# The variance of a channel norm on 64 columns instead of 128, and what spreads it back

## The chip, the core and the metric

The kernel runs on one core of a Trainium2 chip. The core has a TensorE (PE, 128x128 array, with its weight loads shown apart as PEld), a VectorE (DVE), a ScalarE (ACT), a GpSimd (POOL) and a SyncE (SP) that issues transfers. The metric is the time of one execution on the device in microseconds; less is better.

## The reference, cut to what matters

The input x is (4, 64, 32, 32): four images, 64 channels, 1024 positions each. It goes through a convolutional local attention (7x7 windows) on a channel norm of x, is added to x, and the sum goes through a sequence of attention and feed-forward steps on a channel norm of that, and is added again:

```python
def _ln_c(v, eps=1e-06):            # v: (B, C, H, W)
    m = jnp.mean(v, axis=1, keepdims=True)
    s = jnp.var(v, axis=1, keepdims=True)
    return (v - m) / jnp.sqrt(s + eps)
...
x = x + _L0_conv_ref(_ln_c(x), ...)
t = _to_tokens(x)
t = t + _L0_ffn_ref(_ln_t(t), ...)  # _ln_t: the same over the 64 channels of a token, eps 1e-05
```

So both norms are taken over the 64 channels of one position, for 4 x 1024 positions, and all that the change touches is in these two norms.

## The kernel before

**Layout.** The partitions hold 2 x 64 channels: images 0 and 1 in partitions 0 to 63, images 2 and 3 in partitions 64 to 127. The free dimension has 2048 columns (two images of 1024 positions), cut into 4 chunks j of 512 columns. A norm is numbered k = 0 (before the convolution) or k = 1 (before the token steps).

**A norm of one chunk** has seven steps on four engines, tied by semaphores:

1. `centre(j)` on TensorE (L345): one 128x128 product that takes the mean over the channels away, into PSUM bank j.
2. `square(k, j)` on ScalarE (L728, L730): the squares to `sq`, and a copy of the centred values to `xc`.
3. `variance(k, j)` on TensorE (L354): the chunk's 512 columns are cut into 4 slots of 128. Slot s is multiplied with 32 columns of `mean_w` into PSUM partitions 32s to 32s+31, so that the four products stand in four column groups of the array. Of the 32 weight columns 16 are used: 8 repeat the mean over the upper 64 channels and 8 that over the lower; the other 16 are zero. The variances of 2 x 512 positions then lie in a tile of 128 partitions and 128 columns.
4. `root(k, j)` on ScalarE (L734): square root of variance + eps, PSUM to `sq`.
5. `inverse(k, j)` on VectorE (L980): reciprocal in place.
6. `spread(k, j)` on TensorE (L363): four products with selecting weights `spread_w` (one row per slot and half is 1) bring 1/std back to all 64 channels of each half; slots 0 and 1 are taken from partitions 0 to 63 (r = 0), slots 2 and 3 from 64 to 127 (r = 1), and the two r go to different PSUM banks.
7. `scale(k, j)` on VectorE (L986): `h2` = centred values times that, which raises `normed` (k = 0) or `h_ready` (k = 1).

**Order.** The order on each engine is written out by hand. On TensorE, first norm: centre 0, centre 1, variance 0, centre 2, variance 1, spread 0, centre 3, spread 1, variance 2, variance 3, spread 2, spread 3, then `queries_keys` (L410), the biases (L426, L429) and `conv_values` (L417). Variance 2 and 3 reuse the banks of chunks 0 and 1 and wait for their `scale`. Second norm, at the end of the convolution (L516 to L544): ... `mix(1, 15)`, variance 0, centre 3, variance 1, `keep_busy` (three products on idle data, L370), spread 0, spread 1, `keep_busy`, variance 2, `load_next` (the queue reads into registers which step comes next), variance 3, spread 2, spread 3, then the section that the data select; here it is a feed-forward (`up`, L680; `down`, L694), followed by an attention. On VectorE each norm is inverse 0, inverse 1, scale 0, scale 1, inverse 2, inverse 3, scale 2, scale 3. On ScalarE the roots stand between the squares.

**Loads.** `mean_w`, the upper half of x and `spread_w` are issued on SP's queue (L232 to L238), behind them the value weights, `wqk`, the masks and the key table. The lower half of x is issued on ScalarE's queue (L740, L741).

The selecting and averaging weights are written on the host:

```python
    for slot in range(2):
        at = P + 32 * slot + 16 * slot + 8 * h
        mean_mat[rows, at:at + 8] = 1.0 / C
        for j in range(4):
            spread_mat[32 * j + 16 * slot + 8 * h, 2 * j + slot, rows] = 1.0
```

`mean_mat` has a second set of 32 columns (slot = 1) in which the used 16 are the others, and `spread_mat` has the rows for both; before the change only slot 0 of either is used.

Of the kernel before, what the change touches and what calls it, by code (L numbers as in the profile page):

```python
# [25 lines left out]
ACT = mybir.ActivationFunctionType  # L26
X = mybir.AxisListType.X

P = 128
C = 64  # L30
# [24 lines left out]
def build(nc, x, w_qk, w_q, w_v, bias_tables, key_onehot, masks, ident, mean_mat, spread_mat, iotas,  # L55
          attn_mask, ffn_mask, attn_pack, ffn_w1, ffn_pack, out):
    with ExitStack() as ctx:
        def sb(name, shape, dt=F32):
            return ctx.enter_context(nc.sbuf_tensor(name, shape, dt))

        def sem(name):
            return ctx.enter_context(nc.semaphore(name))

        ps = ctx.enter_context(nc.psum_tensor("ps", [P, 8, 512], F32))
# [2 lines left out]
        eye = sb("eye", [P, P])  # L67
        mean_w = sb("mean_w", [P, P + 2 * 32])
        centre_w = sb("centre_w", [P, P])
        spread_w = sb("spread_w", [P, 2, P])  # L70
        idle_in = sb("idle_in", [P, 512])
        masks_xy = sb("masks_xy", [P, WW])
        wqk = sb("wqk", [P, P])
# [14 lines left out]
        sq = sb("sq", [P, COLS])  # L88
# [54 lines left out]
        S = {n: sem(n) for n in names}  # L143
# [86 lines left out]
        @block.sync  # L230
        def _(sp):
            sp.dma_start(mean_w[:], mean_mat).then_inc(S["mean_loaded"], 16)  # L232
            sp.dma_start(x2[0:C, 0], x_parts[0][0]).then_inc(S["x0_loaded"], 16)
            sp.dma_start(x2[0:C, 1], x_parts[1][0]).then_inc(S["x1_loaded"], 16)
            for r in range(2):
                for odd in range(2):
                    sp.dma_start(spread_w[C * r:C * r + C, odd, :],
                                 spread_mat[C * r:C * r + C, 2 * (2 * r + odd), :]).then_inc(S["s_loaded"], 16)  # L238
            sp.wait_ge(S["w_zeroed"], 1)
            for h in range(2):  # L240
                sp.dma_start(wv_bd[C * h:C * h + C, C * h:C * h + C], w_v).then_inc(S["w_loaded"], 16)
            for h in range(2):
                sp.dma_start(wqk[C * h:C * h + C, :], w_qk).then_inc(S["w_loaded"], 16)
            sp.dma_start(masks_xy[:], masks).then_inc(S["c_loaded"], 16)
            for b in range(4):
                sp.dma_start(k_aug[C:P, b, :, :], key_onehot).then_inc(S["c_loaded"], 16)
            sp.wait_ge(S["table_ready"], 1)
            sp.dma_start(next_steps, ahead_i[:]).then_inc(S["table_spilled"], 16)
            sp.wait_ge(S["table_spilled"], 16)
            sp.dma_start(table[:], next_steps.rearrange("p n -> (p n)").unsqueeze(0)  # L250
                         ).then_inc(S["table_loaded"], 16)


            def attention(a, f, ev, row):
                sp.wait_ge(S["fold_d"], a + 1)
                sp.dma_start(wa[:], attn_pack[bass.ds(row, 1)].rearrange("o c k d -> (o c) k d")
                             ).then_inc(S["aw_loaded"], 16)

            def feed_forward(a, f, ev, row):
                sp.wait_ge(S["ffn_done"], f + 1)  # L260
                for h in range(2):
                    sp.dma_start(w1d[C * h:C * h + C, :],
                                 ffn_w1[bass.ds(row, 1)].rearrange("o c k -> (o c) k")
                                 ).then_inc(S["fw_loaded"], 16)
                sp.dma_start(w2p[:], ffn_pack[bass.ds(row, 1)].rearrange("o p k -> (o p) k")
                             ).then_inc(S["fw_loaded"], 16)

            load_next, run, sections = routing(sp)
            load_next()
            run(attention, feed_forward)  # L270

            base = sp.snap(4 * sp.snap(sections()))
            for j in range(4):
                sp.wait_ge(S["summed"], base + j + 1)
                sp.sem_inc(S["passed"], 1)
                for h in range(2):
                    sp.dma_start(o_parts[j // 2][h][:, (j % 2) * 512:(j % 2) * 512 + 512],
                                 osum[C * h:C * h + C, j * 512:j * 512 + 512]).then_inc(S["stored"], 16)
            sp.wait_ge(S["stored"], 16 * 8)
# [62 lines left out]
        def _(pe):  # L342
# [5 lines left out]
            def variance(k, j):  # L348

                pe.wait_ge(S["squared"], 4 * k + j + 1)  # L350
                if j >= 2:
                    pe.wait_ge(S["h_ready" if k else "normed"], j - 1)
                for s in range(4):
                    mm = nc.tensor.matmul(ps[32 * s:32 * s + 32, 4 + 2 * (j % 2), 0:P], mean_w[:, P:P + 32],  # L354
                                          sq[:, j * 512 + P * s:j * 512 + P * s + P], start=True, stop=True)
                mm.then_inc(S["var_ready"], 1)

            def spread(k, j):

                pe.wait_ge(S["inv_ready"], 4 * k + j + 1)  # L360
                for odd in range(2):
                    for r in range(2):
                        mm = nc.tensor.matmul(ps[:, 4 + 2 * (j % 2) + r, P * odd:P * odd + P],  # L363
                                              spread_w[C * r:C * r + C, odd, :],
                                              sq[C * r:C * r + C, j * 512:j * 512 + P], start=True, stop=True)
                mm.then_inc(S["spread_ready"], 1)

            def keep_busy(bank, n):
# [9 lines left out]
            for h in range(2):  # L378
                mm = nc.tensor.matmul(ps[C * h:C * h + C, 7, 0:TX + TY], wq_nat[:], rel_tab[:],
                                      start=True, stop=True)  # L380
# [5 lines left out]
            centre(0)  # L386
            centre(1)
            variance(0, 0)
            pe.wait_ge(S["x1_loaded"], 32)
            centre(2)  # L390
            variance(0, 1)
            pe.wait_ge(S["s_loaded"], 64)
            spread(0, 0)
            centre(3)
            pe.wait_ge(S["tab_copied"], 4)
            spread(0, 1)
            variance(0, 2)
            variance(0, 3)
            spread(0, 2)
            spread(0, 3)  # L400

# [319 lines left out]
        def _(act):  # L721
# [9 lines left out]

            def root(k, j):
                act.wait_ge(S["var_ready"], 4 * k + j + 1)
                nc.scalar.activation(sq[:, j * 512:j * 512 + P], ps[:, 4 + 2 * (j % 2), 0:P], ACT.Sqrt,  # L734
                                     bias=eps_c[:, k:k + 1]).then_inc(S["std_ready"], 1)

            act.dma_start(wq_nat[:], w_q).then_inc(S["t_loaded"], 16)
# [18 lines left out]
            square(0, 0)  # L756
            square(0, 1)
            root(0, 0)
            square(0, 2)
            root(0, 1)  # L760
            square(0, 3)
            root(0, 2)
            root(0, 3)
            act.wait_ge(S["zeroed"], 1)
# [174 lines left out]
        def _(dve):  # L939
# [35 lines left out]

            def inverse(k, j):

                rstd = sq[:, j * 512:j * 512 + P]
                dve.wait_ge(S["std_ready"], 4 * k + j + 1)
                nc.vector.reciprocal(rstd, rstd).then_inc(S["inv_ready"], 1)  # L980

            def scale(k, j, done="normed"):
# [5 lines left out]
                                        ps[:, bank:bank + 2, 0:256], ALU.mult).then_inc(S[done], 1)  # L988

            inverse(0, 0)  # L990
            inverse(0, 1)
            scale(0, 0)
            scale(0, 1)
            inverse(0, 2)
            inverse(0, 3)
            scale(0, 2)
# [317 lines left out]
```

## Time and profile before

| | |
|---|---|
| median of 3 runs | 254.68 us (253.95 to 255.96) |
| the profiled execution, its own time | 256.12 us |
| its span in the trace | 254.3 us |
| TensorE busy | 231.9 us, 91% of the span |
| VectorE, ScalarE, GpSimd busy | 170.4, 160.3, 39.5 us |
| first norm in the trace | about 8 to 19.7 us |
| second norm in the trace | about 92 to 106.6 us |

Times in the trace count from the start of the span. The profiled execution is one execution; it took 1.4 us more than the median of the three timed runs.

### The profile page before, as it was taken

Reading aid. Unit: us, or ns where it says so; the run is one execution under the profiler, and the core shown is the slowest. Engines: PE = TensorE matmul, PEld = TensorE weight load, DVE = VectorE, ACT = ScalarE, POOL = GpSimd, SP = SyncE. Lnnn points to the kernel's source line nnn. Section 1 sums busy time; section 2 is a strip of 40 time slices with the busy share of each in tenths; the row PEclk is TensorE's granted clock in tenths of the full one; section 3 lists DMA queues with packets and bytes.
Section 4 is the critical chain, followed back from the end, with each engine's and each line's share of the span. In section 5 each row is a group of like instructions: output and inputs, shape, how many; then the busy total and the mean of one; then the engine's idle time right before and its main releaser. Section 6 shows DMA issues by size and latency. Waiting matters only on the chain.

```text
span 254.3 us, 5286 instructions
## 1 busy us (share of the span) xinstructions
PE 231.9 (91%) x1814; PEld 158.1 (62%) x1815; DVE 170.4 (67%) x312; ACT 160.3 (63%) x297; POOL 39.5 (16%) x66
## 2 busy tenths in 40 slices
PE   7879972999999999799899999999999999998992
PEld 3346732777787755432375778887777777786330
DVE  0179938677777735464596999897668667761652
ACT  1937754266666694454459988879876666672641
POOL 9900041444445200250000000000000000000000
PEclk9999998599999999799999999999999999999997
DMA  6950000000000001000100000000000000000006
GB/s 162 189 118 3 4 0 1 0 0 3 0 0 0 0 0 31 3 0 10 38 0 0 3 0 0 3 0 3 0 3 3 3 0 3 0 3 0 0 18 149
DMA packets 3302, 4.77 MB, mean 19 GB/s; under 512 B 1041, under 2 KB 2257, under 8 KB 3282
## 3 DMA queue, kind: packets, MB, share of 16 engines
q1 hardware_dynamic: 2758, 3.86, 6.9%
q10 hardware_dynamic: 524, 0.64, 1.1%
q8 instruction: 13, 0.21, 0.4%
q14 instruction: 7, 0.06, 0.1%
HBM read 3.45 MB, written 1.05 MB: 18 GB/s over the span
## 4 chain that ended last, share of the span: by engine, by line
PE 79%; ACT 7%; DVE 7%; issue 4%; DVEq 1%; POOL 0%; ACTq 0%; POOLq 0%
PE ps L613 12%; PE ps L627 11%; PE ps L601 8%; PE ps L451 7%; PE ps L680 6%; PE ps L694 6%; PE ps L483 5%; PE ps L472 5%; ACT arena L903 4%; PE ps L462 2%; PE ps L426 2%; PE ps L345 2%; PE ps L375 2%; PE ps L363 2%; DVE arena L1016 2%
## 5 line engine op out<-in xcount | busy, mean ns | idle before, releaser
L903 ACT COPY arena<-ps 128x1024 f32<-128x1024 f32 x32 | 32.4, 1011 | 20.4 <-PE ps L613 19.3
L1127 DVE TENSOR_REDUCE negmax<-ps 128x1 f32<-128x1024 f32 x32 | 38.7, 1219 | 2.9 <-PE ps L601 2.8
L601 PE MATMUL ps<-h_st,g_st 128*128 128x512 f32 x128 | 38.6, 423 | 0.9 <-DVE h_st L1114 0.5
L852 ACT ACTIVATE pr<-ps,negmax 128x1024 f32<-128x1024 f32 x32 | 35.8, 1119 | 4.2 <-DVE negmax L1127 3.9
L613 PE MATMUL ps<-eye,pr 128*128 128x128 f32 x256 | 33.7, 275 | 2.8 <-ACT arena L903 2.3
L613 PEld LDWEIGHTS ps<-eye,pr 128*128 128x128 f32 x256 | 28.6, 140 | 11.1 <-issue 5.1
L627 PE MATMUL ps<-arena,vk 128*64 128x128 f32 x512 | 31.5, 276 | 1.1 <-ACT arena L903 1.1
L627 PEld LDWEIGHTS ps<-arena,vk 128*64 128x64 f32 x512 | 27.6, 137 | 3.8 <-issue 2.3
L786 ACT ACTIVATE prob<-ps,negmax 128x308 f32<-128x308 f32 x32 | 16.3, 513 | 21.0 <-DVE negmax L1027 21.0
L601 PEld LDWEIGHTS ps<-h_st,g_st 128*128 128x128 f32 x128 | 21.8, 188 | 9.0 <-issue 3.2
L1137 DVE TENSOR_SCALAR pr<-pr,rinv 128x1024 f32<-128x1024 f32 x32 | 24.1, 753 | 1.1
L451 PE MATMUL ps<-arena,q_st 128*128 (+1 forms) x64 | 20.7, 446 | 1.7 <-POOL q_st L306 1.7
L1027 DVE TENSOR_REDUCE negmax<-ps 128x2 f32<-128x616 f32 x16 | 12.8, 799 | 7.9 <-PE ps L451 7.9
L472 PE MATMUL ps<-eye,prob 128*103 128x128 f32 x96 | 14.9, 293 | 2.9 <-DVE prob L1035 2.9
L918 ACT ACTIVATE arena<-ps,w2p 128x512 f32<-128x512 f32 x16 | 11.0, 687 | 9.7 <-PE ps L680 9.7
L680 PE MATMUL ps<-h,w1d 64*128 64x512 f32 x64 | 16.6, 651 | 0.0
L796 ACT COPY prob_t<-ps 103x384 f32<-103x384 f32 x32 | 13.7, 481 | 3.6 <-PE ps L472 2.9
L306 POOL TENSOR_TENSOR q_st<-arena,ones_c 128x128 f32<-128x128 f32 x32 | 12.2, 402 | 24.3 <-ACT arena L778 22.6
L313 POOL TENSOR_TENSOR v_st<-arena,ones_c 128x308 f32<-128x308 f32 x16 | 11.2, 701 | 26.4 <-PE ps L462 26.4
L472 PEld LDWEIGHTS ps<-eye,prob 128*103 128x103 f32 x96 | 11.5, 174 | 6.1 <-issue 6.1
L694 PE MATMUL ps<-arena,w2p 128*64 128x512 f32 x64 | 15.1, 602 | 0.0
L451 PEld LDWEIGHTS ps<-arena,q_st 128*128 128x128 f32 x64 | 11.4, 198 | 5.6 <-issue 2.8
(112 smaller groups left out, 335.3 us busy)
## 6 DMA issues: line engine op xcount, KB each, us to landing
arena<-in_key_onehot SPq DMA_DIRECT2D x4, 361.0 KB, 6.1
out<-tabs SPq DMA_DIRECT2D x8, 128.0 KB, 2.3
x<-in_x SPq DMA_DIRECT2D x2, 256.0 KB, 3.8
x<-in_x ACTq DMA_DIRECT2D x2, 256.0 KB, 5.1
w1d<-in_ffn_w SPq DMA_DIRECT2D x4, 64.0 KB, 2.2
w2p<-in_ffn_pack SPq DMA_DIRECT2D x2, 65.5 KB, 2.1
spread_w<-in_spread_mat SPq DMA_DIRECT2D x4, 32.0 KB, 5.1
mean_w<-in_mean_mat SPq DMA_DIRECT2D x1, 96.0 KB, 2.0
```

Of the source, the lines that this page charges most:

```text
L451: mm = nc.tensor.matmul(ps[:, 2 * xb + h, 0:NKEY], q_st[:, xb, h, :], k_aug[:, bass.ds(2 * h + b2, 1), bass.ds(BR * hb, KR), BC * xb:BC * ...
L472: mm = nc.tensor.transpose(ps[0:CH, 4 + h, c * P:c * P + P], prob[:, pp, h, c * CH:c * CH + CH], eye[:])
L601: mm = nc.tensor.matmul(ps[:, 2 * h + c, :], g_st[:, b2, h, q0:q0 + P], h_st[:, b2, h, part, c * 512:c * 512 + 512], start=(part == 0), st ...
L613: mm = nc.tensor.transpose(ps[:, 4 + c // 4, (c % 4) * P:(c % 4) * P + P], pr[:, n % 2, c * P:c * P + P], eye[:])
L627: mm = nc.tensor.matmul(ps[C * h:C * h + C, 7, cols], vk[:, g // 2, c, C * h:C * h + C], prt[:, g % 2, h, c, cols], start=(c == 0), stop=( ...
L680: mm = nc.tensor.matmul(ps[:, set0 + 2 * h + c, :], w1d[C * h:C * h + C, c * P:c * P + P], h2[C * h:C * h + C, t * 512:t * 512 + 512], sta ...
L694: mm = nc.tensor.matmul(ps[C * h:C * h + C, set0 + first, :], w2p[:, c * C:c * C + C], hid[t % 2][:, 2 * h + c, :], start=(i == 0), stop=( ...
L786: ins = nc.scalar.activation(prob[:, pp, h, 0:NKEY], ps[:, 2 * pp + h, 0:NKEY], ACT.Exp, bias=negmax[:, pp, h:h + 1], accum_out=rowsum[:, ...
L852: nc.scalar.activation(pr[:, n % 2, :], ps[:, 2 * (n % 2):2 * (n % 2) + 2, :], ACT.Exp, bias=negmax[:, 0, n % 2:n % 2 + 1], accum_out=rows ...
L903: nc.scalar.copy(prt[:, n // 8 % 2, n % 2, :, q0:q0 + P], ps[:, 4:6, :].rearrange("p b (c q) -> p (b c) q", c=4)).then_inc(S["s_pt"], 1)
L1127: nc.vector.tensor_reduce(negmax[:, 0, n % 2:n % 2 + 1], ps[:, 2 * (n % 2):2 * (n % 2) + 2, :], mybir.AxisListType.XY, ALU.max, negate=Tru ...
L1137: nc.vector.tensor_scalar(pr[:, n % 2, :], pr[:, n % 2, :], rinv[:, 0, n % 2:n % 2 + 1], None, ALU.mult).then_inc(S["s_prob"], 1)
```

## The change

The variances of a chunk are kept on 64 columns instead of 128. Each of the four slots of 128 positions is cut into two halves of 64. In `variance` both halves go to the same 32 partitions and the same 64 columns of PSUM: half 0 with the weights of slot 0 (which fill 16 of the 32 rows) as the start of an accumulation, half 1 with the weights of slot 1 (the other 16 rows) added to it. So there are eight products of 64 columns instead of four of 128. `root` and `inverse` work on 128x64 instead of 128x128. `spread` has four parts of 64 columns for each of the two r, each with selecting weights of its own: eight products of 64 columns instead of four of 128. `spread_w` grows from [128, 2, 128] to [128, 4, 128] and is loaded by two transfers of 128 KB instead of four of 32 KB.

```diff
--- before.py
+++ after.py
@@ -67,7 +67,7 @@
         eye = sb("eye", [P, P])
         mean_w = sb("mean_w", [P, P + 2 * 32])
         centre_w = sb("centre_w", [P, P])
-        spread_w = sb("spread_w", [P, 2, P])
+        spread_w = sb("spread_w", [P, 4, P])
         idle_in = sb("idle_in", [P, 512])
         masks_xy = sb("masks_xy", [P, WW])
         wqk = sb("wqk", [P, P])
@@ -233,9 +233,8 @@
             sp.dma_start(x2[0:C, 0], x_parts[0][0]).then_inc(S["x0_loaded"], 16)
             sp.dma_start(x2[0:C, 1], x_parts[1][0]).then_inc(S["x1_loaded"], 16)
             for r in range(2):
-                for odd in range(2):
-                    sp.dma_start(spread_w[C * r:C * r + C, odd, :],
-                                 spread_mat[C * r:C * r + C, 2 * (2 * r + odd), :]).then_inc(S["s_loaded"], 16)
+                sp.dma_start(spread_w[C * r:C * r + C], spread_mat[C * r:C * r + C, 4 * r:4 * r + 4, :]
+                             ).then_inc(S["s_loaded"], 16)
             sp.wait_ge(S["w_zeroed"], 1)
             for h in range(2):
                 sp.dma_start(wv_bd[C * h:C * h + C, C * h:C * h + C], w_v).then_inc(S["w_loaded"], 16)
@@ -350,19 +349,22 @@
                 pe.wait_ge(S["squared"], 4 * k + j + 1)
                 if j >= 2:
                     pe.wait_ge(S["h_ready" if k else "normed"], j - 1)
-                for s in range(4):
-                    mm = nc.tensor.matmul(ps[32 * s:32 * s + 32, 4 + 2 * (j % 2), 0:P], mean_w[:, P:P + 32],
-                                          sq[:, j * 512 + P * s:j * 512 + P * s + P], start=True, stop=True)
+                for slot in range(2):
+                    for s in range(4):
+                        at = j * 512 + P * s + C * slot
+                        mm = nc.tensor.matmul(ps[32 * s:32 * s + 32, 4 + 2 * (j % 2), 0:C],
+                                              mean_w[:, P + 32 * slot:P + 32 * slot + 32], sq[:, at:at + C],
+                                              start=(slot == 0), stop=(slot == 1))
                 mm.then_inc(S["var_ready"], 1)
 
             def spread(k, j):
 
                 pe.wait_ge(S["inv_ready"], 4 * k + j + 1)
-                for odd in range(2):
+                for part in range(4):
                     for r in range(2):
-                        mm = nc.tensor.matmul(ps[:, 4 + 2 * (j % 2) + r, P * odd:P * odd + P],
-                                              spread_w[C * r:C * r + C, odd, :],
-                                              sq[C * r:C * r + C, j * 512:j * 512 + P], start=True, stop=True)
+                        mm = nc.tensor.matmul(ps[:, 4 + 2 * (j % 2) + r, C * part:C * part + C],
+                                              spread_w[C * r:C * r + C, part, :],
+                                              sq[C * r:C * r + C, j * 512:j * 512 + C], start=True, stop=True)
                 mm.then_inc(S["spread_ready"], 1)
 
             def keep_busy(bank, n):
@@ -389,7 +391,7 @@
             pe.wait_ge(S["x1_loaded"], 32)
             centre(2)
             variance(0, 1)
-            pe.wait_ge(S["s_loaded"], 64)
+            pe.wait_ge(S["s_loaded"], 32)
             spread(0, 0)
             centre(3)
             pe.wait_ge(S["tab_copied"], 4)
@@ -731,7 +733,7 @@
 
             def root(k, j):
                 act.wait_ge(S["var_ready"], 4 * k + j + 1)
-                nc.scalar.activation(sq[:, j * 512:j * 512 + P], ps[:, 4 + 2 * (j % 2), 0:P], ACT.Sqrt,
+                nc.scalar.activation(sq[:, j * 512:j * 512 + C], ps[:, 4 + 2 * (j % 2), 0:C], ACT.Sqrt,
                                      bias=eps_c[:, k:k + 1]).then_inc(S["std_ready"], 1)
 
             act.dma_start(wq_nat[:], w_q).then_inc(S["t_loaded"], 16)
@@ -975,7 +977,7 @@
 
             def inverse(k, j):
 
-                rstd = sq[:, j * 512:j * 512 + P]
+                rstd = sq[:, j * 512:j * 512 + C]
                 dve.wait_ge(S["std_ready"], 4 * k + j + 1)
                 nc.vector.reciprocal(rstd, rstd).then_inc(S["inv_ready"], 1)
```

## Rows read from the trace of the kernel before

**Rows 1.** The page: busy time and its share, DMA rate in 40 slices.
```profile
PE 231.9 (91%) x1814; PEld 158.1 (62%) x1815; DVE 170.4 (67%) x312; ACT 160.3 (63%) x297; POOL 39.5 (16%) x66
...
GB/s 162 189 118 3 4 0 1 0 0 3 0 0 0 0 0 31 3 0 10 38 0 0 3 0 0 3 0 3 0 3 3 3 0 3 0 3 0 0 18 149
```

**Rows 2.** The chain that ended last, first norm: start us, us, what.
```profile
12.89 0.72 PE ps L363 x8
...
15.43 0.70 DVE h L986
17.14 0.96 DVE sq L980
18.15 0.71 PE ps L363 x8
...
33.98 0.61 ACT arena L778
```

**Rows 3.** The chain that ended last, second norm.
```profile
98.73 1.09 PE ps L363 x16
...
101.67 0.98 issue
...
103.53 0.96 DVE sq L980
...
105.77 4.60 PE ps L680 x16
```

**Rows 4.** Timeline of the second norm.
```profile
96.65 2.00 DVE L980 RECIPROCAL sq<-sq 128x128 f32<-128x128 f32 x2 [0.96 <-ACT sq L734]
...
98.66 1.16 PE L363 MATMUL ps<-sq,spread_w 64*128 64x128 f32 x16
```

**Rows 5.** Timeline of the first norm: start us, us, instructions, idle before.
```profile
10.55 0.30 PEld L345 LDWEIGHTS ps<-x,centre_w 128*128 128x128 f32 x2 [0.20 <-issue]
...
11.61 0.43 PE L354 MATMUL ps<-sq,mean_w 128*32 128x128 f32 x8
...
12.87 0.55 PEld L363 LDWEIGHTS ps<-sq,spread_w 64*128 64x128 f32 x8 [1.10 <-issue]
```

**Rows 6.** Single lines, whole span: minimum, median, maximum in ns.
```profile
L354 PEld LDWEIGHTS ps<-sq,mean_w x64: 106/106/109, 10.2 to 102.7; 128*32 128x32 f32 x64
L354 PE MATMUL ps<-sq,mean_w x64: 269/273/297, 10.2 to 102.8; 128*32 128x128 f32 x64
...
L363 PEld LDWEIGHTS ps<-sq,spread_w x64: 182/188/335, 12.9 to 105.1; 64*128 64x128 f32 x64
...
L734 ACT ACTIVATE sq<-ps,eps_c x8: 367/368/443, 11.4 to 103.1; 128x128 f32<-128x128 f32 x8
...
L980 DVE RECIPROCAL sq<-sq x8: 952/953/954, 11.8 to 103.5; 128x128 f32<-128x128 f32 x8
...
L1134 DVE RECIPROCAL rinv<-rowsum x32: 141/164/165, 132.3 to 227.5; 128x1 f32<-128x1 f32 x32
```

**Rows 7.** Timeline of TensorE in the last group of biases.
```profile
28.31 0.30 PE L426 MATMUL ps<-h,tabs 128*64 128x64 f32 x1
...
28.66 0.22 PE L429 MATMUL ps<-h,tabs 128*64 128x64 f32 x1
...
29.80 0.51 PE L426 MATMUL ps<-h,tabs 128*64 128x64 f32 x3
```

**Rows 8.** DMA issues: KB each, median us from issue to landing.
```profile
x<-in_x ACTq DMA_DIRECT2D x2, 256.0 KB, 5.1
...
spread_w<-in_spread_mat SPq DMA_DIRECT2D x4, 32.0 KB, 5.1
```

**Rows 9.** Three stretches: us, engines' busy time, granted clock (PEclk), DMA share, GB/s.
```profile
43.12:49.95 6.83, 6.06 (x27) 4.70 (x28) 4.44 (x11) 1.11 (x4) 2.90 (x6) 0.50 0.00 0
...
101.30:104.56 3.26, 1.53 (x27) 0.83 (x26) 1.98 (x3) 1.78 (x3) 0.00 (x0) 1.00 0.02 5
104.56:107.98 3.42, 3.42 (x14) 2.02 (x16) 1.16 (x2) 0.90 (x3) 1.33 (x2) 0.50 0.00 0
```

## Prediction, written before the result was known

> **What bounds the kernel now.** I read the page's busy shares first: TensorE is busy for 91% of the span [rows 1], so the kernel is a TensorE stream with some holes. The change touches only the two channel norms, so the question is whether their steps lie on the chain that ends last, and on which engine. In the first norm that chain [rows 2] runs through every kind of step that is edited: square root (L734), reciprocal (L980), spread (L363), then centre(3), spread(0,1), the multiply (L986), variance(0,3), root, reciprocal, and spread(0,3), behind which the queries and keys start at once. From there the chain stays on TensorE until ScalarE's copy at 33.98, so what the first norm ends later by, the kernel ends later by. In the second norm the chain [rows 3] is different: idle products, both spreads 0 and 1 back to back, idle products, a variance, 0.98 us of issue, a variance, root, reciprocal, spread(1,3), and at once the feed-forward (L680). Here two of the four reciprocals are off the path: both are done at 98.65, just when TensorE comes free of idle products [rows 4].
>
> **The records.** A float32 product leaves two matmul records, so variance (4 products) has 8 records and spread (4 products) also 8 [rows 5]; both become 16.
>
> **Reciprocal, 8 of them, 128 to 64 columns.** 953 ns for 128 columns, 164 ns for one [rows 6]: (953 - 164)/127 = 6.2 ns a column, so 64 columns take 164 + 63 x 6.2 = 555 ns. Gain 0.40 us each. This is the only large gain.
>
> **Square root, 8 of them.** 368 ns for 128 columns [rows 6]. Half the columns save between nothing and half of that; the reciprocal's row of one column shows that a call has a fixed part, and ScalarE's is the larger here, so I take 0.04 us each.
>
> **Spread, 8 of them: from 4 products of 128 columns to 8 of 64.** The columns that pass are the same, but the weights are 128 columns wide each time and are loaded twice as often. What a load occupies is seen where two loads of 128 columns stand alone: the record of one is 0.19 long and both together take 0.30 [rows 5, 6], so they start 0.11 apart. The row halves of the array load side by side: eight spread loads take 0.55 in all [rows 5], about 0.19 + 3 x 0.11, four in each half. Products follow their loads: first load 0.11, three more 0.11 apart, the last record 0.27, together 0.71; the chain says 0.72 [rows 2]. Today load (0.11) and product (the record's two halves share 128 columns passed in 0.11 each) are matched; afterwards the product is half as long and the load is not, so the loads set the pace: 0.11 + 7 x 0.107 + 0.22 (the record of a 64-column product [rows 7]) = 1.08. So a spread becomes 0.37 us longer. Ends: 0 if a shorter product brings a shorter load, +0.44 if sixteen records keep the pace of the second norm's sixteen, 1.16 in all [rows 4]. I take +0.37, as the load rows lie on one line whatever is multiplied: 106 ns for 32 columns, 188 for 128 [rows 6], 0.85 ns a column. The Trainium skill says the same ("TensorE: Matmul & The Clock Gate", section "LDWEIGHTS (loading the stationary operand)": a load takes its columns over 1.2 in ns, and the rows don't matter), an estimate of 107 ns here. By that rule, which the trace bears out, the loads cost what the smaller variance saves.
>
> **Variance, 8 of them: 4 products of 128 columns to 8 of 64, accumulated in pairs.** The four column groups run side by side: eight records of 0.27 within 0.43 [rows 5, 6], so starts are 0.02 apart. Each group then does four halves instead of two wholes. Expected +0.05; bounds 0 and +0.5 (rival B).
>
> **First norm, step by step** [rows 2, 5]. root(0,0) ends 0.04 earlier, its reciprocal runs 11.75 to 12.30, and spread(0,0) starts 0.14 behind that, as now: 12.44 to 13.52 instead of 12.89 to 13.61. The 0.45 won is spent again. centre(3) ends 0.09 earlier, at 14.58. spread(0,1) 14.51 to 15.59 (now it ends 0.11 before the multiply at 15.43): the reciprocal of this chunk has long been ready, so only the longer spread counts. The multiply ends at 16.41 (now 16.13). reciprocal(0,2) 16.41 to 16.97, variance(0,3) 16.54 to 16.97, root to 17.32, reciprocal(0,3) 17.35 to 17.90 (now 17.14 to 18.10). spread(0,2) starts at 17.03 and holds TensorE for 1.02, so spread(0,3) starts at 18.05 (now 18.15) and ends at 19.13, where it now ends at 18.86. Result: +0.27 us. The reciprocals' gains are met by three longer spreads, and the last reciprocal runs beside a spread.
>
> **Second norm** [rows 3, 4]. Both first spreads start at 98.66 as now, since idle products hold TensorE until then. They take 2 x 0.37 = 0.74 more, and the idle products and variance(1,2) move by that. Then PE's queue reads the routing registers (0.98 of issue). If that begins when the variance is through, variance(1,3) moves by 0.74; if it is timed from the first multiply, which moves by 0.36, by less. Root and reciprocal give back 0.44, and spread(1,3) takes 0.37: +0.3 to +0.7. I take +0.65 with the small cost of the variances in it.
>
> **The loads.** spread_w is fetched in 2 issues instead of 4 on SP's queue, and with twice the bytes. What stands behind it on that queue (the value weights, wqk, the masks, the key table) is issued earlier and nothing in the chain waits for it: nothing. What lands beside it is x's lower half from ScalarE's queue, issued at 2.7 and 3.2 and landed 5.1 later [rows 8], at 7.8 and 8.3, for centre(0), which starts at 8.4, and centre(2), at 10.55 [rows 5]. 128 KB more at the 162 to 189 GB/s of these slices [rows 1] are 0.7 to 0.8 us, of which x bears a part. So the cover of 0.6 may just hold; it costs 0, and up to 0.3 if it doesn't. spread_w lands by about 9.5 at the latest, for a use at 12.4.
>
> **Sum.** +0.27 + 0.65 = +0.9 us. The profiled execution took 256.12 (span 254.3 and 1.8 around it) and would take 257.0. It stands 1.4 above the median of 254.68, so the forecast for the median is 255.6. One reason for the spread of 2 us between runs stands in the rows: the granted clock was full from 101.30 to 104.56, where TensorE was busy for 1.53 of 3.26 us, and then half, 1.2 GHz, until 107.98 [rows 9]. That spell costs about half its length on the path, 1.7 us, and an execution without it would stand near the lower runs.
>
> **Rival A: loads get cheaper with the products.** Then a spread stays at 0.72 and the reciprocals on the path are won: 0.45 at spread(0,0) and 0.45 more behind it in the first norm, 0.45 once in the second. Together -1.35: 253.3. Against it: the loads that start 0.11 apart. 10%.
>
> **Rival B: each matmul takes a slot of its own however short it is.** The shortest products in a long stream are the biases, 64 columns with 64 columns of weights: 32 records whose first starts at 28.31 and whose last at about 30.0, 55 ns apart [rows 7]. If that is a floor, sixteen variance records hold TensorE for 0.88 instead of 0.36. The first norm pays 0.45 for it before its last reciprocal, and in the second norm all four variances stand in TensorE's chain: 2.0. With the +0.9 that makes +3.4: 258.1, slower by 1.3%. It decides as soon as a record costs more than 0.36/16 = 22 ns. The Trainium skill has such a rule (same page, section "Back-to-back issue gap": a small matmul occupies about 62 ns where its queue decodes it in software, and about 25 otherwise). For less than 55: the variance's own records, 0.02 apart; and half of the biases read with a stride, with records of 0.30 against 0.22 [rows 7], which explains their pace. 10%.
>
> **Rival C: the clock.** If the longer spreads fill the quiet stretch before 104.56 so that the clock doesn't fall, the 1.7 come back: +0.9 - 1.7 = -0.8, or 253.9. For it: TensorE would be busy 1 us more there. 12%. The other way, a second spell, or one as long as that of 43.12 to 49.95 [rows 9], adds 1.7: 257.3, 8%. The stretch between the idle products and L680 stays about 4 us long, so I expect neither.
>
> **Chances and range.** The forecast's own case has 60%, from 254.6 to 256.6 by the bounds above and the runs' scatter. Eight in ten: 253.2 to 257.4, which leaves out B and the ends of A and C. A measurement of this kernel can't tell less than about 1% (2.5 us) from no change. Slower by over 1% (above 257.2): B and some of the longer spell, 13%. Faster by over 1% (below 252.1): A together with a lost spell, 3%. Within 1%: 84%.
>
> **What would show it.** In the profile after: reciprocals of 64 columns at 0.55; a spread's sixteen matmul records in about 1.08 with its loads 0.11 apart in each row half (the step is right), or in 0.72 (A); variance's sixteen records within 0.5 (right) or near 0.9 to 1.1 (B); spread(0,3) ending near 19.1; L680 starting 0.7 later than 105.77; the granted clock around 104 to 108 (C). The forecast is wrong in sign if the loads are hidden, and in size if the variances' records go one by one.

## The result, and the profile after

The changed kernel takes 257.75 us (median of 7, 256.60 to 258.34), the kernel before 254.45 in the same series (median of 7, 253.75 to 256.15). The ratio is 1.0117, 95% interval 1.0081 to 1.0154: slower by 3.0 us by the ratio (the medians lie 3.3 apart), where +0.9 was forecast and 253.2 to 257.4 given as the range. In the series below a few executions took 299 to 1226 us; the medians count them, the ratios do not. The profiled execution took 258.34 with a span of 256.5, 2.2 more than that of before.

The page of the changed kernel, first the busy shares, then the granted clock in 40 slices, then the two DMA rows that stood in [rows 8]:

```profile
PE 234.7 (92%) x1942; PEld 161.8 (63%) x1943; DVE 168.0 (66%) x312; ACT 160.1 (62%) x297; POOL 39.5 (15%) x66
...
PEclk9999998699999999889999999999999999999998
...
x<-in_x ACTq DMA_DIRECT2D x2, 256.0 KB, 7.2
spread_w<-in_spread_mat SPq DMA_DIRECT2D x2, 128.0 KB, 6.6
```

TensorE is 2.8 us busier [rows 1], and both kinds of transfer land later. The edited lines, minimum, median and maximum in ns, beside [rows 6]:

```profile
L355 PE MATMUL ps<-sq,mean_w x128: 216/219/243, 11.2 to 105.0; 128*32 128x64 f32 x128
...
L365 PEld LDWEIGHTS ps<-sq,spread_w x128: 182/188/188, 13.4 to 107.0; 64*128 64x128 f32 x128
L365 PE MATMUL ps<-sq,spread_w x128: 272/272/320, 13.4 to 107.1; 64*128 64x64 f32 x128
...
L736 ACT ACTIVATE sq<-ps,eps_c x8: 314/316/393, 12.3 to 105.3; 128x64 f32<-128x64 f32 x8
...
L982 DVE RECIPROCAL sq<-sq x8: 553/553/553, 12.7 to 105.6; 128x64 f32<-128x64 f32 x8
```

The reciprocal is 553 ns (forecast 555), the root 316. The record of a spread's load is still 188 ns long, and there are 128 of them now. The chain of the first norm, beside [rows 2]:

```profile
2.68 6.47 DMA x<-in_x
...
13.41 1.11 PE ps L365 x16
...
16.74 0.70 DVE h L988
...
17.57 0.43 PE ps L355 x16
...
18.00 2.12 PE ps L365 x32
20.12 1.77 PE ps L412 x8
```

It begins with a transfer: x's lower half, issued at 2.68, landed at 9.15, and centre(0) starts at 9.28 instead of 8.4. A spread is 1.11 instead of 0.72, and the last two stand back to back in 2.12. The chain of the second norm, beside [rows 3]:

```profile
99.14 1.93 PE ps L365 x32
101.07 1.49 PE ps L372 x6
102.57 0.36 PE ps L355 x16
102.93 1.88 issue
104.81 0.43 PE ps L355 x16
105.24 2.12 PE ps L365 x32
107.36 5.19 PE ps L682 x16
```

The pair of spreads takes 1.93 instead of 1.09, and the gap before variance(1,3) 1.88 instead of 0.98 ("issue": time for which the profile shows nothing that TensorE waited for). The granted clock behind it, in two stretches, beside [rows 9] (columns as there):

```profile
102.56:107.31 4.75, 2.87 (x67) 2.53 (x68) 1.79 (x3) 2.11 (x4) 0.00 (x0) 1.00 0.02 3
107.31:110.72 3.41, 3.41 (x12) 1.39 (x12) 1.10 (x2) 0.69 (x1) 2.47 (x3) 0.51 0.00 0
```

By stage, from the timelines of both profiled executions:

| stage | before | after | difference |
|---|---|---|---|
| start to centre(0) | 8.39 | 9.28 | +0.89 |
| first norm, to the first L410 / L412 | 10.31 | 10.68 | +0.37 |
| convolution, to centre(1) of the second norm | 73.87 | 73.02 | -0.85 |
| second norm, to the first L680 / L682 | 12.99 | 14.21 | +1.22 |
| from there to the end | 148.72 | 149.29 | +0.57 |

The convolution did not get faster: its spell at half clock began at 42.45 and ended at 49.28 here, and at 43.12 to 49.95 before, when the same steps are 1.3 us later here, so more of it fell on time in which TensorE waited anyway (it was busy for 5.49 us of the spell here and for 6.06 before). Single executions differ by such things, so what follows rests on paired series and, for places, on the traces. Each execution's mean granted clock also says how long it ran at half clock, 2 x (1 - clock) x span; I call this half-clock time. It averages 9.0 to 9.8 us in the three series of the kernel before that stand beside the experiments, and 11.8 in the changed kernel's. Within each of those three, a line through the executions gives 0.2 to 0.3 us of time for each us of half-clock time.

### The profile page after: what moved, and what is told of

It is laid out like the page before. It is cut to its first block, busy times and chain, and to the rows that moved or that the text cites. A ratio compares the mean times of both kernels' runs of the same rounds, so it can differ in the third digit from the quotient of the medians.

```text
span 256.5 us, 5540 instructions
## 1 busy us (share of the span) xinstructions
PE 234.7 (92%) x1942; PEld 161.8 (63%) x1943; DVE 168.0 (66%) x312; ACT 160.1 (62%) x297; POOL 39.5 (15%) x66
## 4 chain that ended last, share of the span: by engine, by line
PE 77%; ACT 7%; DVE 6%; issue 5%; DMA 3%; ACTq 1%; DVEq 1%; POOL 0%; POOLq 0%
PE ps L615 11%; PE ps L629 11%; PE ps L603 8%; PE ps L453 7%; PE ps L682 6%; PE ps L696 6%; PE ps L485 5%; PE ps L474 5%; ACT arena L905 4%; PE ps L365 3%; DMA x<-in_x 3%; PE ps L464 2%; PE ps L344 2%; PE ps L428 2%; DVE arena L1018 2%
## 5 line engine op out<-in xcount | busy, mean ns | idle before, releaser
L905 ACT COPY arena<-ps 128x1024 f32<-128x1024 f32 x32 | 32.4, 1012 | 20.3 <-PE ps L615 19.3
L682 PE MATMUL ps<-h,w1d 64*128 64x512 f32 x64 | 17.2, 671 | 0.0
```

Source lines behind the costliest of these rows:

```text
L682: mm = nc.tensor.matmul(ps[:, set0 + 2 * h + c, :], w1d[C * h:C * h + C, c * P:c * P + P], h2[C * h:C * h + C, t * 512:t * 512 + 512], sta ...
L905: nc.scalar.copy(prt[:, n // 8 % 2, n % 2, :, q0:q0 + P], ps[:, 4:6, :].rearrange("p b (c q) -> p (b c) q", c=4)).then_inc(S["s_pt"], 1)
```

## The experiments

The first theory had three parts: (1) spreads paced by their weight loads, (2) instructions of the longer variance that hold up PE's queue before it reads the routing registers, (3) x held up by the loads of spread_w. Rivals were that the gap came from the later multiply, and that the late x was chance.

**The spread alone.** Kernel before, with

```diff
-                for odd in range(2):
+                for part in range(4):
                     for r in range(2):
-                        mm = nc.tensor.matmul(ps[:, 4 + 2 * (j % 2) + r, P * odd:P * odd + P],
-                                              spread_w[C * r:C * r + C, odd, :],
-                                              sq[C * r:C * r + C, j * 512:j * 512 + P], start=True, stop=True)
+                        at = j * 512 + C * (part % 2)
+                        mm = nc.tensor.matmul(ps[:, 4 + 2 * (j % 2) + r, C * part:C * part + C],
+                                              spread_w[C * r:C * r + C, part // 2, :],
+                                              sq[C * r:C * r + C, at:at + C], start=True, stop=True)
```

> The kernel before with only the spread cut: eight products of 64 columns, each with its own load of 128 weight columns, nothing else changed. Theory (the weight loads set the pace, and each extra product costs its load): a spread takes 1.1 us instead of 0.72. All eight are on the path here, because the reciprocals stay at 0.95: first norm +0.4 three or four times (spread(0,3) ends 1.2 to 1.6 later), second norm +0.85 for the pair and +0.4 for the last; sum +2.3 to +2.9 us, 256.8 to 257.3 against 254.5. x arrives as before (centre(0) at 8.4). Rival (a load is as cheap as its product): spreads stay at 0.72 and the time at 254.5.

Measured: 257.80 (median of 6), ratio 1.0122 (1.0080 to 1.0163). The chain of its first norm:

```profile
12.91 1.11 PE ps L364 x16
14.02 1.07 PE ps L345 x2
...
16.23 0.69 DVE h L987
...
16.94 0.96 DVE sq L981
...
17.95 2.74 PE ps L364 x32
```

The spread takes 1.11 with 128-column reciprocals beside it, as in the changed kernel: the rival is out. The last pair takes 2.74 instead of the 2.12 above. The reason is the clock, in four stretches of that time, and in one of the changed kernel:

```profile
17.00:18.00 1.00, 0.48 (x10) 0.24 (x10) 0.94 (x2) 0.37 (x1) 0.00 (x0) 1.00 0.00 0
18.00:19.00 1.00, 1.00 (x18) 0.96 (x18) 0.90 (x1) 0.00 (x0) 0.00 (x0) 1.00 0.06 16
19.00:20.00 1.00, 1.00 (x14) 1.00 (x14) 0.69 (x1) 0.00 (x0) 0.00 (x0) 0.63 0.00 0
20.00:22.00 2.00, 2.00 (x12) 1.27 (x12) 1.14 (x4) 0.00 (x0) 0.00 (x0) 0.50 0.00 0
```

```profile
19.00:20.00 1.00, 1.00 (x20) 0.99 (x18) 0.69 (x1) 0.00 (x0) 0.00 (x0) 1.00 0.00 0
```

It fell near 19.3 although both TensorE rows say 1.00 busy, behind a microsecond with TensorE busy for 0.48. The changed kernel ran the same products in the same place at full clock.

The second norm grew by only 0.39 (13.38 against 12.99), where +1.25 was expected. Its timeline, and below it the multiplies of the kernel before:

```profile
101.49 0.69 DVE L987 TENSOR_TENSOR h<-xc,ps 128x512 f32<-128x512 f32 x1 [1.23 <-PE ps L364]
...
104.72 0.43 PE L354 MATMUL ps<-sq,mean_w 128*32 128x128 f32 x8 [0.61 <-issue]
```

```profile
99.49 1.28 DVE L986 TENSOR_TENSOR h<-xc,ps 128x512 f32<-128x512 f32 x2 [0.84 <-PE ps L363]
```

Variance(1,3) starts 3.23 behind the start of the first multiply, and 3.16 behind it in the kernel before (at 102.65). So with variances of eight records variance(1,3) keeps its distance from the first multiply, and part of what the spreads take longer goes into a shorter gap, 0.61.

**Sixteen products per spread.** The same edit with 16 products of 32 columns.

> The kernel before with each spread as sixteen products of 32 columns, so the same columns in all and four times the weight loads of before. Theory (107 ns for a load of 128 columns in each row half, whatever is multiplied): 0.11 + 15 x 0.107 + 0.2 = 1.9 to 2.0 us for a spread of 32 records, loads 0.11 apart in each half. Rival (0.37 more per spread was a fixed cost of the first doubling, or the queue's decoding of instructions sets the pace): a spread of 1.1 to 1.5, or well over 2.0. In all +5 to +7 us on one look.

One execution: 272.57. The first spread in TensorE's timeline:

```profile
13.26 1.98 PE L364 MATMUL ps<-sq,spread_w 64*128 64x32 f32 x32 [0.86 <-DVE sq L981]
```

0.11 + 15 x 0.107 + 0.27 = 1.98: the rule for the load (107 ns for 128 columns in each row half, whatever is multiplied) holds to 2%, over 4, 8 and 16 products (0.71, 1.13 and 1.98 by the rule with a last record of 0.27; 0.72, 1.11 and 1.98 measured). The total rose by 18 us and not by 5 to 7: I had not reckoned with the clock, which was half for 10 us from the third spread on (next rows; the spreads end at 27.07, queries and biases follow) and for 10 more in the second norm. Here too TensorE had been busy for less than half of the time just before.

```profile
18.50:20.00 1.50, 0.47 (x12) 0.19 (x8) 1.45 (x2) 0.73 (x2) 0.00 (x0) 0.99 0.00 0
20.00:30.00 10.00, 9.97 (x72) 8.01 (x72) 4.11 (x14) 0.96 (x2) 0.00 (x0) 0.50 0.00 0
```

**The variance alone.** Kernel before, with

```diff
-                for s in range(4):
-                    mm = nc.tensor.matmul(ps[32 * s:32 * s + 32, 4 + 2 * (j % 2), 0:P], mean_w[:, P:P + 32],
-                                          sq[:, j * 512 + P * s:j * 512 + P * s + P], start=True, stop=True)
+                for half in range(2):
+                    for s in range(4):
+                        at = j * 512 + P * s + C * half
+                        mm = nc.tensor.matmul(ps[32 * s:32 * s + 32, 4 + 2 * (j % 2), C * half:C * half + C],
+                                              mean_w[:, P:P + 32], sq[:, at:at + C], start=True, stop=True)
```

> The kernel before with only the variance cut: eight products of 64 columns instead of four of 128, no accumulation, nothing else changed. Theory (sixteen records still pass in 0.43, but PE's queue needs time for each instruction, and that shows only where the queue itself is behind): each variance stays at 0.43; the issue gap between variance(1,2) and variance(1,3), now 0.98, grows to about 1.9; the kernel is slower by 0.9. Rival 1 (the gap of 1.88 in the changed kernel comes from the later multiply before it): the gap stays at 0.98 and the time at 254.5. Rival 2 (rival B of the prediction): each variance takes 0.9, and the kernel is slower by 2.4.

Measured: 257.62 (median of 12), ratio 1.0087 (1.0056 to 1.0118), +2.2 us. The chain of its second norm:

```profile
99.98 1.49 PE ps L372 x6
101.47 0.36 PE ps L356 x16
101.83 1.86 issue
103.70 0.47 PE ps L356 x16
...
104.18 0.38 ACT sq L736
```

The gap is 1.86 with nothing else changed, and the variance itself still passes in 0.36 on the chain, 0.43 in its records. So rival 1 (the multiply) and rival 2 (the array) both fall for this growth: it comes from the number of records. Variance(1,2) has sixteen more, eight of products and eight of weight loads, so 0.88 us is 55 ns for each record of either kind, or 110 for each product record. That is a quotient for this place and not a rate of the queue: in the changed kernel's first norm variance(0,3) waits for the multiply that ends at 17.44, and all its 32 records are through by 18.00 (unless the queue reads records ahead of a wait, which the profile does not show). From centre(1) to the first feed-forward record the second norm takes 13.88 instead of 12.99, +0.9. The measured +2.2 is more, and half-clock time says where the rest may be: 13.9 us on average against 9.8 in the executions of before beside it. In the profiled one a spell of 6.8 us begins 1.1 us behind the end of the longer gap, where before one of 3.4 began 1.9 behind it [rows 9].

**The loads alone.** Kernel before, with the changed kernel's two transfers into a spread_w of four parts, of which parts 0 and 2 are used.

```diff
-                for odd in range(2):
-                    sp.dma_start(spread_w[C * r:C * r + C, odd, :],
-                                 spread_mat[C * r:C * r + C, 2 * (2 * r + odd), :]).then_inc(S["s_loaded"], 16)
+                sp.dma_start(spread_w[C * r:C * r + C], spread_mat[C * r:C * r + C, 4 * r:4 * r + 4, :]
+                             ).then_inc(S["s_loaded"], 16)
```

> The kernel before with only the loads of the changed kernel: spread_w as two transfers of 128 KB, of which the spread reads parts 0 and 2 (the old weights). Theory (the larger and earlier transfers on SP's queue hold up x's lower half): x's lower halves land 6.5 and 8 us after their issue instead of 4.7 and 5.5, centre(0) starts at 9.3 instead of 8.4, the first norm ends 0.9 later and the kernel is slower by about 0.9. Rival (x was late by chance in the one profiled execution): centre(0) at 8.4 and 254.5.

Measured: 254.91 (median of 12), ratio 1.0001 (0.9968 to 1.0033). Its DMA rows and TensorE's timeline:

```profile
x<-in_x ACTq DMA_DIRECT2D x2, 256.0 KB, 6.1
spread_w<-in_spread_mat SPq DMA_DIRECT2D x2, 128.0 KB, 6.1
```

```profile
6.90 1.98 PE L382 MATMUL ps<-idle_in 128*128 128x512 f32 x4
8.72 1.88 PE L344 MATMUL ps<-x,centre_w 128*128 128x512 f32 x4
```

x's lower halves land 1.0 later than in [rows 8], but centre(0) follows the idle products (6.90 to 8.88) without a wait. It starts 0.33 later than before because the idle products do. So part 3 of the theory holds for the transfers and fails for the time: the landing is later, the cover mostly holds. In the changed kernel's profiled execution it did not.

**Bytes or order of issue.** The changed kernel with spread_w in four issues of 64 KB; the kernel before with two issues of 64 KB:

> The changed kernel with spread_w in four transfers of 64 KB instead of two of 128 KB: the bytes of the changed kernel, but the issues behind them on SP's queue are back at their old times. If the 1.2 us of earlier issue (the value weights, wqk and the masks compete with x) did the harm, x lands as before and centre(0) starts at 8.4 to 8.6. If the 128 KB did it, centre(0) stays near 9.3. I expect the bytes to count for more: about 9.0.

> The kernel before with spread_w in two transfers of 64 KB instead of four of 32 KB: the bytes of before, but what stands behind is issued 1.2 us earlier. The counterpart of the run with four issues: centre(0) at 8.4 to 8.7 if the bytes did the harm (time 254.5 to 254.8), at 9.3 if the earlier issue did (255.4).

Four issues: 256.96 (median of 6), ratio 1.0103 (1.0042 to 1.0163), x's lower halves landed in 6.4 (median, by the page), centre(0) at 8.84. Two issues of the old bytes: 254.64 (median of 12), ratio 0.9984 (0.9955 to 1.0013), landed in 5.6, centre(0) at 8.19. The runs with the old loads land x in 5.1 to 5.5, so the bytes delay it, and the earlier issues alone (5.6) not visibly. Neither difference can be told from none in the time.

**x ahead of spread_w.** The changed kernel, with SP waiting for the first part of x:

```diff
+            sp.wait_ge(S["x0_loaded"], 32)
             for r in range(2):
                 sp.dma_start(spread_w[C * r:C * r + C], spread_mat[C * r:C * r + C, 4 * r:4 * r + 4, :]
```

> The changed kernel with one wait more on SP's queue: spread_w and all that stands behind it are issued only when both halves of the first part of x have landed. Theory (x is held up by what SP issues beside it): centre(0) starts at 8.4 or earlier again instead of 9.3, and the kernel gains 0.9 on the changed one: 256.8 against 257.7. What may come late instead: spread_w, issued near 7 and landed near 11, for a use at 12.4; if it needs more than 5.4 us, spread(0,0) waits and the gain is lost. Rival (x is late for its own queue's reasons): centre(0) stays at 9.3.

Measured: 257.75 (median of 6), ratio 1.0129 (1.0086 to 1.0172). centre(0) starts at 7.78, and the time is that of the changed kernel all the same. Six executions from 256.1 to 259.7 with a half-clock time of 13.3 can't tell 0.9 us, so the order is neither shown to help nor shown not to.

**The change without its longer spread.** Kernel before with the changed variance, root and reciprocal, and

```diff
-                                              sq[C * r:C * r + C, j * 512:j * 512 + P], start=True, stop=True)
+                                              sq[C * r:C * r + C, j * 512:j * 512 + C].unsqueeze(1).broadcast_to([C, 2, C]),
+                                              start=True, stop=True)
```

> The kernel before with variance, root and reciprocal of the changed one (64 columns), its loads as before, and the spread as four products of 128 columns that read the 64 columns twice (half of the positions so get the standard deviation of another position; that part of the computation is changed). It is the change without its longer spreads and without its loads. Theory: reciprocals at 0.55 and spreads at 0.72, the first norm ends 0.9 earlier than before; in the second norm the reciprocal gives 0.45 and the issue gap takes 0.9 back. Sum -0.4 to -0.5: 254.0. If the queue's gap did not come from the variance, -1.35: 253.1. If the reciprocals were never on the path, +0.5 to +0.9.

Half of the positions get the deviation of another position here, so this kernel shows the time only. Measured: 253.96 (median of 12), ratio 0.9962 (0.9935 to 0.9989), about -1.0. The chain of its first norm:

```profile
11.70 0.56 DVE sq L984
...
12.40 0.71 PE ps L366 x8
...
16.60 0.56 DVE sq L984
...
17.21 0.71 PE ps L366 x8
17.92 1.72 PE ps L414 x8
```

spread(0,0) starts at 12.40 and L414 (the queries) at 17.92 instead of 18.87: the reciprocals were on the path, worth 0.9 here, when the spread stays at 0.71. The second norm still has its gap, 1.96, and takes 13.34 instead of 12.99, so the two norms together give about -0.6, near the -0.4 to -0.5 expected. Half-clock time is 9.1 in spite of the gap. This is what the change would bring if spreading cost no more than before.

**The routing registers read early.** In the changed kernel and in the kernel before the same move:

```diff
             centre(1)
             centre(2)
+            load_next, run, sections = routing(pe)
+            load_next()
             mix(1, 15)
...
             variance(1, 2)
-            load_next, run, sections = routing(pe)
-            load_next()
             variance(1, 3)
```

> The changed kernel with PE's reading of the routing registers moved ahead of mix(1, 15), where two centre products keep the array busy while the queue reads. Theory (the gap of 1.88 before variance(1,3) is the queue's: instructions of variance(1,2), then the registers): the gap shrinks to the wait for the second multiply, variance(1,3) starts about 1.5 to 2 us earlier, the last reciprocal and spread with it, and the kernel gains 1.0 to 1.9: 255.9 to 256.7 against 257.7. If the registers are not the gap, it only moves and nothing is gained.

> The kernel before with PE's reading of the routing registers moved ahead of mix(1, 15), as in the changed kernel's run of that name. There the gap went from 1.88 to nothing, the second norm became 1.03 shorter and half-clock time fell. Theory: here the gap of 0.98 goes, variance(1,3) is then held by the second multiply (100.77 and 0.14) or by variance(1,2) (101.6), so it starts about 1.0 earlier, and with it root, reciprocal and the last spread; the stretch with little TensorE work gets shorter by the same, so fewer executions lose clock. 253.4 against 254.7. Rival (the gain there was clock alone): same span at the same granted clock, 254.2 or so.

Changed kernel: 255.56 (median of 12), ratio to before 1.0018 (0.9996 to 1.0041). TensorE's timeline:

```profile
100.55 1.56 PE L372 MATMUL ps<-idle_in 128*128 128x256 f32 x6
102.04 0.65 PE L355 MATMUL ps<-sq,mean_w 128*32 128x64 f32 x32
103.49 2.00 PE L365 MATMUL ps<-sq,spread_w 64*128 64x64 f32 x32 [0.80 <-DVE sq L982]
105.33 1.08 PE L682 MATMUL ps<-h,w1d 64*128 64x512 f32 x4
```

Both variances stand together in 0.65, the gap is gone, and from centre(1) to the first feed-forward record the norm takes 13.18 instead of 14.21. That is 1.0; the median fell by 2.2. The rest goes along with half-clock time: 7.3 us instead of 11.8. In the kernel before, the move brought the norm from 12.99 to 12.55 and gave 254.53 (median of 12), ratio 0.9979 (0.9952 to 1.0006), with a half-clock time of 9.9 beside 9.0 for before. I expected 1.0 to 1.3 less. The gap is gone there too, but the two reciprocals of 0.95 then stand back to back on VectorE (102.57 to 104.33 on its chain) and take the gap's place.

**Both remedies.** In the kernel before and in the changed one:

> The kernel before with the registers read early and with spread_w and what follows it on SP's queue issued only when the first part of x has landed. Theory: centre(0) starts at 7.8 instead of 8.4 as in the changed kernel with that order, and the gain of the early registers comes on top: 252.8 to 253.2. If the start's gain is lost again in the convolution (its chain has a fixed start for another reason), the same time as with the early registers alone.

> The changed kernel with both remedies: registers read early, x ahead of spread_w. Theory (of the change's +3, one part each was the queue's gap with its clock and the late x, and the longer spreads remain): 254.7 to 255.2, still slower than the kernel before with the same two remedies by 1.5 to 2: the narrower reciprocals don't pay for the loads of the weights. Rival (the change is good once the two are out of its way): as fast as that one or faster.

Before with both: 254.72 (median of 12), ratio 0.9994 (0.9971 to 1.0018), where 252.8 to 253.2 was expected: centre(0) starts at 8.28, behind the idle products, hardly earlier than 8.39. Changed with both: 255.68 (median of 12), ratio 1.0040 (1.0019 to 1.0062), with a half-clock time of 8.7 beside 9.0 for before. This is the change with its gap and late x taken out and the clock nearly even: +1.0 us, against the kernel before and against that kernel with both remedies. In the profiled executions of the two kernels with both remedies the first norm takes 10.69 and 10.31, the second 13.17 and 12.64: +0.9, the longer spreads less the shorter reciprocals. No version that computes the norms in full is clearly faster than the kernel before.

## Why the prediction was wrong

- **Reciprocal and root: right.** 553 and 316 ns against 555 and about 330.
- **Spread: right.** 1.11 against 1.08, with a last record of 0.27 where 0.22 was taken, and the sixteen products bear out the load rule. Rival A is out.
- **First norm: right.** +0.37 against +0.27, with the same order of steps.
- **Variance: the array's part right, the cost wrong.** The block stays at 0.43, as forecast. But "Expected +0.05" counted only the array. With twice the records in variance(1,2) the gap between it and variance(1,3), where the queue also reads the routing registers, grows by 0.88 (0.98 with the cheap spread), and without the register reads there it is gone. What the queue does in that time stays open.
- **Second norm: this is the step that failed.** It said "+0.3 to +0.7" and that variance(1,3) moves by 0.74 at most; it moved by 1.75 relative to centre(1) (from 10.08 to 11.83 behind it), and the norm grew by 1.22. Three parts make the 1.75. The first multiply starts 0.41 later (7.33 instead of 6.92 behind centre(1)), as its spread is longer; the run with the spread alone shows that variance(1,3) follows it. The records of the variance add 0.88. The last 0.46 stays open: variance(1,3) starts 4.50 behind the first multiply here and 4.04 in the run with the variance alone. The first multiply, from the changed kernel's timeline:

```profile
100.31 0.69 DVE L988 TENSOR_TENSOR h<-xc,ps 128x512 f32<-128x512 f32 x1 [1.69 <-PE ps L365]
```

- **The sum without that step: near.** With the registers read early and x first in both kernels the change costs 1.0, and 0.9 by its two norms, the 0.9 of the forecast. That bears the sum out only in part: the first norm takes the forecast's path, the second another one, without the gap.
- **Rival B: not it.** It charged all variances to the array at 55 ns for each product record. They pass as fast as before, and only one gap pays. That pays 110 for each product record, and 55 only if weight loads are counted too, so the likeness of the two numbers is no evidence for it. The Trainium skill's figure ("TensorE: Matmul & The Clock Gate", section "Back-to-back issue gap") is about 62 ns for each small matmul decoded in software. No run here bears it out: the gap grows by 110 for each product record, and variance(0,3) of the first norm sends its sixteen within 0.56 us of the multiply that it waits for, 35 each. If the queue had read them ahead of that wait, the second number says nothing.
- **The loads: a size too small, without effect.** x's lower halves land 1 to 2 us later; the ratio with the loads alone is 1.0001. In the changed kernel's profiled execution centre(0) did wait, and started 0.89 later. The forecast took both lower halves to land 5.1 behind their issue. That was the median of two: they took 4.7 and 5.5 in the kernel before, 6.5 and 8.0 in the changed one, and centre(0) waits for the first.
- **The clock: underrated.** Rival C's bad side got 8%. Half-clock time rose from about 9.5 to 11.8 on average; at the 0.2 to 0.3 us for each us of the series that is an estimated 0.5 to 0.7, and at half speed at most 1.1. It is a likely part of the remainder of 3.0 - 0.37 - 1.22 - (0 to 0.9 of late x). What raised it is not shown. The variance alone has 13.9, and in the changed kernel the move of the registers brought it to 7.3, which points at the gap. But the cheap spread has the longest gap (1.96) and 9.1, the spread alone has a shorter gap than before (0.61) and 12.6, and in the kernel before the move of the registers left it at 9.9.

## What to carry to other kernels

Cutting the columns of a product from 128 to 64 or 32 saved nothing on TensorE here while its weights stayed 128 columns wide: each product then cost its loads, two of 0.107 us in its part of the array, and doubling the products doubled that. Count records as well as time in the array: a block that passed in 0.36 before and after lengthened the gap behind it by 0.9, at a place where the queue also had registers to read, and reading them elsewhere took the gap away. And ask what the time won is met by: with the gap gone, the kernel before waited for its two reciprocals instead.

## What the runs showed of the hardware

A product with 128 columns of weights took as long with 64 or 32 columns as with 128: spreads of 4, 8 and 16 such products took 0.72, 1.11 and 1.98 us, about 0.1 us for each product more.

The granted clock fell to half in stretches where the TensorE rows show it busy all the time: near 19.3 in the run with the spread alone, and from 20.0 to 30 in the one with sixteen products. In both TensorE had been busy for less than half of the time before these stretches (0.48 us of 17.00 to 18.00 in the first, 0.47 us of 18.50 to 20.00 in the second). The changed kernel had 0.43 us of 17.00 to 18.00, then the same 64-column products as the first of them, and stayed at full clock. So the busy shares of the page did not tell whether the clock would hold, and these runs don't show what decided it.
